# GpSimd's scatter of scaled rows in an attention stage: one tile in every slot instead of two tiles in every second slot

## What is computed

```python
x = x + attention(layernorm(x))      # 8 heads, low-rank queries, keys and values
x = x + experts(layernorm(x), ctx)   # 8 experts, hidden 512, top 2 by logits of ctx @ Wg + bg
x = x + experts2(layernorm(x))       # 32 experts, hidden 64, top 8 of 4 groups, and 2 shared ones

# the first expert layer
scores_topk, idx_topk = top_k(ctx @ Wg + bg, 2)
weights = softmax(scores_topk)
h = relu(einsum('bsd,edf->bsef', x, W1) + b1)
y = einsum('bsef,efd->bsed', h, W2) + b2
out = einsum('bsed,bse->bsd', y, combine)
```

## Time and profile before

| | us |
|---|---|
| median of three runs | 680.75 (679.41 to 681.75) |
| the profiled execution | 684.1 |
| its span, first to last instruction | 682.2 |
| TensorE busy in the span | 625.1 (92%) |
| VectorE busy | 533.3 (78%) |
| ScalarE busy | 422.4 (62%) |
| GpSimd busy | 345.8 (51%) |
| mean granted clock of TensorE | 0.959 of full speed |

### The profile page before, as it was taken

The page is one execution under the profiler, slowest core; times in us unless marked ns, Lnnn a source line. Parts: engine busy times, 40 slices in busy tenths (PEclk is TensorE's granted clock), DMA queues, the critical chain, the costliest instruction groups (busy, mean ns, idle before and its releaser), DMA issues.

```text
span 682.2 us, 11547 instructions
## 1 busy us (share of the span) xinstructions
PE 625.1 (92%) x3354; PEld 467.1 (68%) x3354; DVE 533.3 (78%) x1357; ACT 422.4 (62%) x779; POOL 345.8 (51%) x410
## 2 busy tenths in 40 slices
PE   8878888888859999989999799999999999999997
PEld 8645555655648887768777456777777767677873
DVE  4787787877975666876674587999999999989973
ACT  3675657765467998869975434563836566484530
POOL 6134767678766567856467654471817356000000
PEclk9988777889898999989999999999999999999999
DMA  8998022002342545544327615443635444444661
GB/s 222 312 383 229 16 87 68 26 28 64 108 144 85 183 152 181 180 134 142 112 71 175 146 46 144 129 128 108 160 102 153 114 131 136 116 121 104 160 158 31
DMA packets 77836, 90.20 MB, mean 132 GB/s; under 512 B 15361, under 2 KB 44011, under 8 KB 77774
## 3 DMA queue, kind: packets, MB, share of 16 engines
q1 hardware_dynamic: 72648, 80.96, 41.4%
q0 software_dynamic: 4288, 8.40, 4.4%
q10 hardware_dynamic: 838, 0.11, 0.1%
HBM read 64.48 MB, written 24.90 MB: 131 GB/s over the span
## 4 chain that ended last, share of the span: by engine, by line
PE 58%; DVE 12%; issue 6%; POOL 5%; ACT 4%; another core or an unknown queue 3%; DMA 1%; DVEq 0%; SPq 0%; ACTq 0%; POOLq 0%
PE bank L1644 8%; PE bank L1646 8%; PE bank L1645 8%; PE pair_banks L1937 6%; PE pair_banks L1546 5%; PE score_banks L1644 4%; PE score_banks L1646 3%; PE score_banks L1645 3%; PE pair_banks L1644 2%; PE pair_banks L1646 2%; PE pair_banks L1645 2%; DVE t_s L1452 1%; POOL x_sorted L619 1%; PE pair_banks L1731 1%
## 5 line engine op out<-in xcount | busy, mean ns | idle before, releaser
L981 ACT ACTIVATE r_s<-bank 128x512 f32<-128x512 f32 x136 | 80.8, 595 | 69.3 <-PE bank L1646 56.2
L1452 DVE TENSOR_TENSOR t_s<-rc_s,bcb 128x512 f32<-128x512 f32 x128 | 89.6, 703 | 4.8 <-PE pair_banks L1937 4.8
L619 POOL DMA_INDIRECT x_sorted<-xsb,posi x64 | 63.9, 999 | 35.8 <-DVE xsb L1248 21.0
L694 POOL DMA_INDIRECT yg<-y_sorted,posi x64 | 68.7, 1073 | 18.1 <-issue 17.9
L1439 DVE TENSOR_TENSOR rc_s<-r_s,score_banks 128x512 f32<-128x512 f32 x90 | 61.2, 680 | 19.7 <-ACT r_s L981 15.7
L1644 PE MATMUL bank<-fxh,Gh 128*128 128x512 f32 x136 | 73.2, 538 | 0.0
L746 ACT ACTIVATE t_h<-t_s 128x512 fp32r<-128x512 f32 x72 | 45.4, 630 | 42.3 <-DVE t_s L1452 27.6
L1937 PE MATMUL pair_banks<-t_s,Dn 128*128 128x512 f32 x128 | 63.1, 591 | 0.0
L1511 DVE TENSOR_TENSOR t_l<-t_s,t_h 128x512 fp32r<-128x512 f32 x72 | 53.8, 747 | 0.2
L1646 PE MATMUL bank<-fxh,Gl 128*128 128x512 f32 x136 | 53.7, 395 | 0.0
L1645 PE MATMUL bank<-fxl,Gh 128*128 128x512 f32 x136 | 53.4, 392 | 0.0
(11 more groups left out here) (335 smaller groups left out, 1847.5 us busy)
## 6 DMA issues: line engine op xcount, KB each, us to landing
bcb<-c_rows SPq DMA_DIRECT2D x128, 256.0 KB
wraw<-in_L_xattn_W SPq DMA_DIRECT2D x46, 256.0 KB
x_sorted<-wraw SPq DMA_DIRECT2D x1, 5888.0 KB, 18.6
y_sorted<-wraw SPq DMA_DIRECT2D x1, 5888.0 KB, 33.7
xg<-x_sorted SPq DMA_DIRECT2D x23, 256.0 KB
y_sorted<-ysb SPq DMA_DIRECT2D x23, 256.0 KB
ctxb<-in_ctx SPq DMA_DIRECT2D x8, 256.0 KB, 5.6
out<-x_all SPq DMA_DIRECT2D x8, 256.0 KB
```

Source lines behind the costliest of these rows:

```text
L619: pool.indirect_dma_start(out=xs, out_offset=bass.IndirectOffsetOnAxis(ap=posi[:, m, c:c + 1], axis=0), in_=xsb[:, m % SC, :], in_offset=N ...
L694: pool.indirect_dma_start(out=yg[:, j % 2, t, c, :], out_offset=None, in_=ys, in_offset=bass.IndirectOffsetOnAxis(ap=posi[:, j * TPS + t, ...
L981: act.activation(r_s[:, n % RB2, :], bank[n % 3][:, :], ACT.Silu).then_inc(F["act"], 1)
L1452: tt(t_s[:, n % TB2, :], rc_s[:, n % CB2, :], bcb[:, p - 1, :], ALU.mult).then_inc(F["t"], 1)
```

## The change

In GpSimd's loop over the slots, tiles below SINGLE = 22 are scattered one in each slot, tile n-9 in slot n. So even tiles keep their place, and odd tiles, which stood right behind them, move to the end of the next, even slot, behind its normalisation and its power. From tile 22 on the order is the old one. No other engine's program changes.

```diff
 LATE = NT - 8
+SINGLE = LATE - 2
 LEAD = 12
...
                 if 0 <= o < LATE and o % 2 == 1:
                     rstd_pair(o)
-                if 0 <= e < NT and e % 2 == 0:
+                if 0 <= e < SINGLE:
+                    scatter(e)
+                if SINGLE <= e < NT and e % 2 == 0:
                     scatter(e)
                     if LATE <= e + 3 < NT:
                         rstd_pair(e + 3)
```

## The result

The changed kernel took **677.24 us** (median of 20 runs, 673.36 to 683.2), the kernel before, run beside it, 682.09 (20 runs). The ratio is 0.9953, with a 95% interval of 0.9930 to 0.9976: faster by 0.5%, or 3.2 us by the ratio (1.6 to 4.8) and 4.85 by the medians. Forecast were 675.3 us and a gain of 5.5. The sign was as forecast, and the waits that were to vanish did; but the gain is little more than half of the forecast one, since VectorE paid for the new order what the sum had put at nothing, and the gain turned out to exist in some series only.

What follows compares the result with a forecast made beforehand. It took the stretch from 105.1 to 175.6 us to be bound by engines waiting for each other. 5.0 us from the eight pairs and the earlier pairs' share made 6.1, taken as 5.5: 675.3 us, range 671.5 to 682.5 (0.8).

Steps and rivals of the forecast that it cites:

- the sum: Eight pairs from 70.5 to 65.5 us, 5.0 gained; with the three earlier pairs 6.1 together, taken as 5.5.
- What bounds the kernel: From 105.1 to 175.6 us GpSimd, VectorE and TensorE are 76% to 84% busy, none full; their mutual waits bind.
- Step 1: GpSimd's own work: its floor stays 8.0 us a pair, 7.97 against 7.99 before, costed at nothing.
- Step 2: GpSimd's normalisation behind the burst: queued behind two issues instead of four, it comes 2.5 us earlier.
- Step 3: GpSimd's queue behind the moved issues: 1.9 us of slack hide the other normalisation; idle time, 1.3 a pair, absorbs the issues.
- Step 4: Buffer of scaled rows: tile m+1 leaves a slot later, 8 us remain before rewriting; cost nothing.
- Step 5: VectorE's 11.0 us of waits before the maximum over the scores, in the eight pairs, all but go.
- The waits stay: Rival: VectorE's waits before the maximum don't come from burst length, pairs stay 8.8 us; 679 to 681.5 us; chance 0.21.
- The waits double: Rival: VectorE waits before the maximum in both slots of a pair; 5.6 us lost, 686.4 us; chance 0.15.
- The issues get dearer: Rival: GpSimd's sixteen moved issues cost the worst, 1.365 us each; 6.4 us lost, 681 us; chance 0.04.
- The clock adds: Rival: TensorE's clock stays up where the expert stage begins, 204 to 210 us; 2.8 us more, 672.5 us; chance 0.10.
- The marks set beforehand: Signs in the trace for right or wrong: pair spacing, idle before the maximum, GpSimd's and TensorE's waits, gain lost after 176 us.

Runs made afterwards that it cites:

- after: The changed kernel, tiles below 22 scattered one a slot, against the kernel before; first measurement 677.24 us, ratio 0.9953.
- level 682: The three series (one chip each, kernels run alternately with the unchanged kernel) in which the unchanged kernel took 681.2 to 682.1 us.
- level 672: The three other series, in which the unchanged kernel took 671.6 to 671.8 us.
- before: The unchanged kernel, four scatter issues in a row in every second slot; 682.09 us in the first measurement.
- before_act_later: The kernel before with the scaling of sorted rows moved from VectorE to ScalarE, issued a slot later; 679.38 us, ratio 1.0098.
- before_again: The kernel before, unchanged, run once more for a second trace, at level 672; 672.61 us, ratio 1.0003.
- after_third: The changed kernel, run once more as a neighbour for other runs, at level 682; 678.27 us, ratio 0.9935 to before.
- norm_waits_late: The changed kernel with GpSimd's normalisation waiting in every second slot, from tile 6 on, until VectorE has scaled both tiles; 673.77 us, ratio 0.9878 to before.
- after_again: The changed kernel, run once more, at level 672; 672.74 us, ratio 0.9993 to before.
- norm_waits_again: The changed kernel with GpSimd's normalisation waiting in every second slot until VectorE has scaled both tiles, repeated; 673.98 us, ratio 0.9893 to before.
- late_singles: The changed kernel with one scatter a slot only for tiles 6 to 21, tiles 0 to 5 in pairs; 671.95 us, ratio 0.9995 to before.
- early_singles: The changed kernel with one scatter a slot only for tiles 0 to 5, pairs from tile 6 on; 672.12 us, ratio 1.0008 to before.

## Why the prediction was wrong in its size, and what it had right

The step that failed is the third, and through it the sum. The prediction let the moved issues use up GpSimd's idle time at no cost to any other engine. The runs show that VectorE had been working undisturbed in that time: in after, the same instructions of VectorE take 6.6 us more in the eight pairs, and these take 67.05 us instead of the 65.5 of the sum. With the normalisation made to wait for VectorE they take 63.6. A second thing failed beside it: the waits that were to vanish are there at level 682 alone, so at level 672 there was nothing to gain. The steps in turn:

**What bounds the kernel.** Three engines between 76% and 84%, bound by how they wait for each other: right for the trace of before. The reading of the 8.9 us without a releaser as tied to the run of four issues held at level 682 (11.0 to 0.6 us by the change, 9.0 where the four stayed) and nowhere else. That they would be there in every series I never questioned, and one trace couldn't have told.

**Step 1, GpSimd's floor at 7.97 us.** Nearly right: 7.79. The 1.41 us from the normalisation to the next scatter, which I took as an issue's own cost, had a wait for the scaled rows in it; with the rows there it is 1.21.

**Step 2, the normalisation comes 2.5 us earlier.** The direction is right and before_act_later shows the cost of the old place, 2.04 us of TensorE at once. That the old order can't keep 8.0 us pairs except by slack from slow ones stays open: before_again has four of eight between 7.99 and 8.00 us, but three of them follow a pair of 8.7 us or more, and TensorE's weight loads waited 9.5 us for normalisations in these eight pairs. After's waits for it fell little over the run at level 682 (6.9 to 6.4).

**Step 3, what stands behind the moved issues is hidden.** This is the step that failed, by an omission. I listed what is queued behind the moved issues on GpSimd, and said that GpSimd's idle time is what they use up. I didn't ask what ran on VectorE during that idle time, and what GpSimd, no longer idle, does to it. It cost VectorE 6.6 us, which I had at nothing. (The end of the normalisation comes to 10.2 us by the terms given, not 10.3; nothing hangs on it.)

**Step 4, the buffers.** Right: VectorE has no idle time before line 1251 in the eight pairs of after.

**Step 5, the waits before the maximum all but go.** Right where they exist: 0.6 us. The nearest row was partly luck: the 0.3 us of the earlier trace rows are from a stretch with gathers two at a time, while from 354 to 379 us of the same trace, where up to eight gathers stand in a row, TensorE's updates were up to 3.1 us late.

**The sum.** Here is the mis-sized term. "The other six go to 8.0, the two long pairs to 17.5" took VectorE's own work as fixed, 16.3 of 19.4 us in the long pairs. It grew by 6.6 us in the eight pairs, by the five groups above. The two long pairs came to 9.19 + 9.79 = 18.98 instead of 17.5, one pair to 8.72 instead of 8.0, and the others to 7.8 to 8.0: 67.05 instead of 65.5, a gain of 3.5 instead of 5.0. With most of the hold-up taken away the same pairs are 8.14, 8.55 and 7.95 (norm_waits_late), and the eight 63.6: my sum would have been too cautious. The first three pairs were to give 1.1 us and gave -0.3 in the profiled run and, in after_third, 0.4 (29.75 against 30.1); of the loss 0.54 us is one stretched instruction of the routing's plan, 0.28 in before and 0.82 in after:

```profile
90.37 0.82 DVE L1176 SCALAR_TENSOR_TENSOR chosen<-order,mine,uses 128x64 f32<-128x64 f32 x1
```

So 3.2 to 3.9 us instead of 6.1, which is what the ratio shows (3.2).

**The rivals.** "The waits stay" is refuted at level 682 and is the outcome at level 672, by another road: they weren't there. "The waits double" is refuted: 0.6 us. "The issues get dearer" named the right contention and the wrong victim: the issues cost 0.999 us on average against 0.985, 0.5 us for 32, and the powers 0.9 us for eight, while VectorE's instructions lost 6.6. The Trainium skill (SBUF — State Buffer, section Who interferes with whom) has it: VectorE and GpSimd share a pair of SBUF ports as an exclusive lock, `tensor_scalar` in its two-port mode and instructions with two SBUF inputs need it, and the one that comes later waits for the whole of the other. The trace agrees that such instructions wait, and for the whole of the other, with 1.86 us for a scaling of 0.34. It doesn't agree on the order: by its row the scaling (139.71) came 0.72 us ahead of the normalisation (140.43) that it waited for. "The clock adds" didn't come. The drop that it was about is still there in after:

```profile
202.00:208.00 6.00, 6.00 (x18) 4.77 (x17) 1.92 (x3) 2.73 (x5) 4.82 (x5) 0.54 0.32 101
```

That is 0.54 where the earlier trace rows has 0.53. In the stage itself it isn't shown to have gained anything: in the eight pairs the granted clock was 1.00 instead of 0.88, and TensorE busy 53.5 us instead of 59.1, but at level 672 it was 0.97 in after_again and 0.91 in before_again with no gain in time.

**The marks set beforehand.** First scatters 8.0 to 8.2 apart in most pairs: five of eight at 7.8 to 8.0, three at 8.7 and more. Idle before the maximum at 3 us or less: yes. The wait for scaled rows below 4 us: no, 5.0. The wait for the normalisation falls from 6.9 us: yes, but only to 6.4. The gain lost between 176 and 204 us: in part, since after is 3.1 us ahead of before at the last maximum (174.5 against 177.6) and 2.3 at the first activation of the expert stage (195.9 against 198.2), counting from a start that was 1.5 us behind.

## What to carry over

An engine's idle time may be someone else's right of way: before filling it, list what the other engines do in it, and whether they share more than semaphores with the engine that is filled. When a change makes busy time grow on an engine whose program it doesn't touch, look there first, by shape, for instructions that got longer. And a wait that the profile can't name may not belong to the kernel: trace the unchanged kernel in a second series before building on it.

## What the runs showed of the hardware

Some of VectorE's fp32 instructions with all operands in SBUF were held up by GpSimd: the scaling (128x128, 0.34 us alone) took up to 1.91 us beside a normalisation and, in all seventeen cases of 1.67 us and more, ended within 0.1 us after it, although it had started first: at 139.71 it started 0.72 us ahead of the normalisation, while an issue was running, and the normalisation went ahead of it. Additions of 128x512 took up to 2.30 us instead of 0.69 (before_act_later), and the addition of a constant to 128x2 elements took up to 1.64 instead of 0.17 (norm_waits_again). One of 1.52, in norm_waits_late, spans the end of an issue and a whole normalisation:

```profile
135.54 1.52 DVE L1325 TENSOR_SCALAR mva<-mva 128x2 f32<-128x2 f32 x1
...
134.97 0.97 POOL L620 DMA_INDIRECT x_sorted<-xsb,posi  x1 [0.30 <-issue]
135.97 1.05 POOL L604 TENSOR_TENSOR sm<-sm,rden 128x512 f32<-128x512 f32 x1
```

An issue of an indirect DMA held scalings up too, but only at its end: a pair of scalings that started 0.08 us after an issue's start took 0.59 us (133.70, norm_waits_late), one that started 0.29 us after it 0.71 and ended 0.02 us behind it (102.95). Fourteen scalings that would have ended in the last 0.2 us of an issue ended 0.02 to 0.03 us behind it instead, with 0.38 to 0.57 us; those that could end 0.3 us ahead of it or earlier, with no normalisation ready behind it, took 0.34. Reductions of 128x512 and 128x256, statistics of 128x128 with their operands in SBUF, and 128x512 instructions with an operand in PSUM kept their times in every trace (0.68, 0.41, 0.28 and 0.69).

From 75 to 176 us TensorE's finished products were noticed late, by up to 3.1 us, during four indirect DMA issues in a row and the normalisation behind them in the series at level 682, by up to 1.7 us and much more rarely during two in a row, and never in those at level 672. One trace shows both: after has 8 such cases, of 1.0 us at most, in the 101 us of the new order, and 9, of up to 2.4 us, in the 34 us behind them, where the old order stands. Why series differ, and whether it is the length of the run of issues or the place of the moved ones that counts, stays open: the kernels that were to separate these (late_singles, early_singles) ran at level 672.
